# A recommender tower on one core: tile 1's shifted copies of x made on chip like tile 0's, and a new order of the first tiles' loads, turns and lookups

## What is computed

```python
e = stack([tbl_f[ids[:, f]] for f in range(32)], axis=1)       # 1024 x 32 x 16
x0 = h = e
for i in range(3):                                             # W0 128x1024, W1 and W2 128x2048
    z = (x0[:, :, None, :] * h[:, None, :, :]).reshape(B, F * G, E)
    y = relu(einsum('oc,bce->boe', W[i], z) + b[i][None, :, None])
    if i != 2: keep, h = y[:, :64], y[:, 64:]
    else:      keep = y
    xs.append(keep)
z = sum(concatenate(xs, axis=1), axis=2)                       # 1024 x 256
h = concatenate([z, dense_ctx], axis=1)
h = maximum(h @ W_top1 + b_top1, 0); h = maximum(h @ W_top2 + b_top2, 0)
y = h @ W_top3                                                 # 1024 x 1
```

## Time and profile before

| | us |
|---|---|
| median of 3 timed runs | 1061.19 |
| lowest, highest | 1061.14, 1063.73 |
| the profiled execution | 1066.62 |
| its span | 1064.8 |
| TensorE busy in it | 995.8 |
| VectorE busy | 821.8 |
| GpSimd busy | 816.3 |
| ScalarE busy | 474.4 |

### The profile page before, as it was taken

How to read it: one execution, slowest core, us unless ns; L and a number is a source line. 1 busy time by engine, 2 the same in 40 slices (tenths; PEclk the granted TensorE clock), 3 DMA queues, 4 the chain that set the end, 5 groups by cost and what they waited for, 6 DMA issues and landing times.

```text
span 1064.8 us, 11324 instructions
## 1 busy us (share of the span) xinstructions
PE 995.8 (94%) x3089; PEld 572.8 (54%) x3089; DVE 821.8 (77%) x750; ACT 474.4 (45%) x595; POOL 816.3 (77%) x524
## 2 busy tenths in 40 slices
PE   3178899999999999999999999999899999999988
PEld 2133455555555555555555555555455555555565
DVE  6234877798778977899778977898778977788882
ACT  2222544444544454454444454444444454543443
POOL 7655779887998879887998789886998766566540
PEclk9579999999999999999999999999999999999989
DMA  8089999989888888899888888888888888889000
GB/s 158 10 189 198 205 199 190 210 191 197 191 194 191 191 192 185 192 198 208 191 194 186 194 188 190 187 192 191 195 187 188 192 186 192 190 186 219 30 1 0
DMA packets 49012, 185.45 MB, mean 174 GB/s; under 512 B 17570, under 2 KB 22178, under 8 KB 28388
## 3 DMA queue, kind: packets, MB, share of 16 engines
q1 hardware_dynamic: 40804, 183.15, 78.2%
q0 software_dynamic: 8192, 2.11, 2.0%
HBM read 182.06 MB, written 3.15 MB: 174 GB/s over the span
## 4 chain that ended last, share of the span: by engine, by line
POOL 42%; PE 26%; issue 18%; DMA 7%; DVE 4%; ACT 2%; SPq 0%; POOLq 0%; ACTq 0%; DVEq 0%
POOL low L500 24%; POOL looked_up L490 16%; PE y L617 15%; PE y L625 6%; DMA looked_up<-in_tbl,ids_now 4%; PE y L640 3%; POOL tail_parts L508 2%; DMA spread<-xcols 2%; DVE unsplit L1070 1%; DVE prod L1070 1%; DMA xcols<-xrows 0%; ACT emb L793 0%; ACT tail_high L853 0%; PE y L721 0%; DVE acc_kept L1101 0%
## 5 line engine op out<-in xcount | busy, mean ns | idle before, releaser
L500 POOL TENSOR_TENSOR low<-unsplit,high 128x1024 fp32r<-128x1024 f32 x221 | 525.1, 2388 | 113.3 <-ACT high L829 111.5
L617 PE MATMUL y<-prod,w1T 128*128 128x512 f32 x1024 | 480.3, 597 | 5.4 <-ACT kept L821 2.7
L1070 DVE TENSOR_TENSOR prod<-spread,h 128x1024 f32<-128x1024 f32 x288 | 349.1, 1216 | 118.3 <-PE y L617 102.6
L829 ACT CAST high<-unsplit 128x1024 fp32r<-128x1024 f32 x224 | 234.0, 1045 | 243.6 <-DVE unsplit L1070 243.2
L1070 DVE TENSOR_TENSOR unsplit<-spread,h 128x1024 f32<-128x1024 f32 x224 | 272.1, 1215 | 48.8 <-ACT h L815 48.6
L490 POOL DMA_INDIRECT looked_up<-in_tbl,ids_now x256 | 248.7, 971 | 69.1 <-issue 59.4
L617 PEld LDWEIGHTS y<-prod,w1T 128*128 128x128 f32 x1024 | 193.5, 192 | 166.8 <-issue 144.1
L625 PE MATMUL y<-high,w2T_high 128*128 128x512 f32 x448 | 226.7, 506 | 4.4 <-ACT high L829 4.4
L640 PE MATMUL y<-low,w2T_high 128*128 128x512 f32 x448 | 202.7, 533 | 6.3 <-POOL low L500 6.3
L625 PE MATMUL y<-high,w2T_low 128*128 128x512 f32 x448 | 177.9, 397 | 0.0
L815 ACT ACTIVATE h<-y,bias 64x512 f32<-64x512 f32 x128 | 83.3, 651 | 209.2 <-PE y L617 208.3
(11 more groups left out here) (115 smaller groups left out, 441.3 us busy)
## 6 DMA issues: line engine op xcount, KB each, us to landing
spread<-xcols SPq DMA_DIRECT2D x128, 1024.0 KB, 9.0
shifted<-xcols SPq DMA_DIRECT2D x124, 256.0 KB
shifted_tail<-xcols SPq DMA_DIRECT2D x124, 64.0 KB
looked_up<-in_tbl,ids_now POOLq DMA_INDIRECT x256
xcols<-xrows SPq DMA_DIRECT2D x32, 96.0 KB, 2.0
spread<-in_L_rec_W SPq DMA_DIRECT2D x3, 512.0 KB, 7.0
spread<-in_L_rec_W SPq DMA_DIRECT2D x1, 1024.0 KB, 11.6
wt<-in_W_top SPq DMA_DIRECT2D x2, 512.0 KB, 8.7
```

Of the source, the lines that this page charges most:

```text
L500: pool.tensor_tensor(low[kind][r][:, :, :], unsplit[kind][r][:, :, :], high[kind][r][:, :, :].bitcast(F32), ALU.subtract).then_inc(s_low[k ...
L617: last = pe.matmul(y[:, :], w, z[:, c, :], start=(n == 0 and c == 0), stop=(item in (LAST0, LAST1) and c == ITEM - 1))
L829: act.copy(high[kind][r][:, :, :], unsplit[kind][r][:, :, :]).then_inc(s_high[kind], 1)
L1070: dve.tensor_tensor(z, x[:, ITEM * n:ITEM * (n + 1), :], b[:, :].unsqueeze(1).to_broadcast([P, ITEM, COLS]), ALU.mult).then_inc(s_made[kin ...
```

## The change

- Tile 1's `shifted` and `shifted_tail` are made like tile 0's: VectorE rotates, TensorE turns, ScalarE copies, between slots -1 and 0. Tile 2 is the first whose shifted copies come back from DRAM.
- SyncE stores x of tile 1 ahead of tile 0's last spread group, and x of tile 2 between tile 1's first two groups.
- In slot 0 the items (0, 0), TAIL and (0, 1) come earlier, and x of tile 2 is turned after (1, 4) instead of after the last item.
- GpSimd's first tail part comes after four of the eight lookups instead of after all; the second slot's tail part keeps eight ahead of it in all, and the 16 that follow stand in one piece.
- In every fourth slot one lookup moves from before the low part of (2, 5) to after it.
- TensorE turns the identity 8 times ahead of each group of w2, and in a loop 16 times 8 times after the weights are stored. The dense features are turned and stored ahead of w2's groups instead of behind them.

```diff
+IDLE_TURNS, IDLE_LOOPS = 8, 16
...
 EARLY = {-1: [TAIL, (0, 0), (0, 1)],
-         0: [(1, 0), (1, 1), (1, 2), (1, 3), (1, 4), (0, 0), TAIL, (1, 5), (0, 1), (1, 6), (1, 7)]}
+         0: [(1, 0), (1, 1), (0, 0), (1, 2), TAIL, (1, 3), (0, 1), (1, 4), (1, 5), (1, 6), (1, 7)]}
+TURN_AFTER = {-1: (0, 1), 0: (1, 4)}
...
-LOOKUPS_AFTER = ((0, 0, 2, 0, 1, 2, 3), (0, 0, 1, 1, 1, 2, 2))
+LOOKUPS_AFTER = ((0, 0, 2, 0, 0, 3, 3), (0, 0, 1, 1, 1, 2, 2))
 LOOKUPS_FIRST = (0, 1)
+LOOKUPS_BEFORE_TAIL = 4
...
-        unwrapped = flat(spread[1][:, 3:4, :])[:, 0:QUAD * XROWS]
-        rotated = [spread[1][:, 4 + c, :] for c in range(GROUP + 1)]
-        first_shifted = [y1, y2[0], y2[1], h1, h0[1]]
+        FIRST_AT = (3, 9)
+        unwrapped = [flat(spread[1][:, n:n + 1, :])[:, 0:QUAD * XROWS] for n in FIRST_AT]
+        rotated = [[spread[1][:, n + 1 + c, :] for c in range(GROUP + 1)] for n in FIRST_AT]
+
+        first_shifted = [[y1, y2[0], y2[1], h1, h0[1]], [y2[1], h1, h0[1], y2[0], y2[0]]]
         FIRST_ORDER = [GROUP, 0, 1, 2, 3]
...
-            def load_shifted(t):
-
-
+            def store_x(t):
                 sp.wait_ge(s_xrows, number(t) + 1)
                 sp.dma_start(xcols[number(t)], xrows[:, :]).then_inc(s_xcols, 16)
...
             def load_factors(t):
+                store_x(t)
                 load_shifted(t)
-
-                if not isinstance(t[0], int) or number(t) >= 1:
-                    load_spread(after(t, -1), GROUPS - 1)
+                load_spread(after(t, -1), GROUPS - 1)
...
             sp.wait_ge(s_stored, PREP_GROUPS)
-            load_factors((0, 0))
+            store_x((0, 0))
+            sp.wait_ge(s_xcols, 16)
+            for g in range(GROUPS - 1):
+                load_spread((0, 0), g)
+            store_x((0, 1))
+            load_spread((0, 0), GROUPS - 1)
 
             sp.wait_ge(s_dense_parts, 1)
 
-            sp.wait_ge(s_first, len(FIRST_ORDER))
-            load_factors((0, 1))
-            load_factors((0, 2))
+            sp.wait_ge(s_first, 2 * len(FIRST_ORDER))
+            sp.wait_ge(s_xcols, 16 * 2)
+            load_spread((0, 1), 0)
+            store_x((0, 2))
+            load_spread((0, 1), 1)
+            load_shifted((0, 2))
+            for g in range(2, GROUPS):
+                load_spread((0, 1), g)
+            for g in range(GROUPS - 1):
+                load_spread((0, 2), g)
...
             begin(1)
-            for f in range(FIELDS // TILES_PER_BLOCK):
+            for f in range(LOOKUPS_BEFORE_TAIL):
                 look_up(f)
-            for k in range(-1, START):
+            split_tail((0, -1))
+            for f in range(LOOKUPS_BEFORE_TAIL, FIELDS // TILES_PER_BLOCK):
+                look_up(f)
+            split_tail((0, 0))
+            for f in range(FIELDS // TILES_PER_BLOCK, 3 * FIELDS // TILES_PER_BLOCK):
+                look_up(f)
+            for k in range(1, START):
                 slot((0, k))
...
+            def turn_dense():
+                pe.wait_ge(s_dense, 16 * 2 * P // COPY)
+                for b in range(BLOCKS):
+                    last = pe.transpose((y0, y1)[b // GROUP][:, P * (b % GROUP):P * (b % GROUP + 1)], dense_wide[:, b, :],
+                                        ident[:, :])
+                last.then_inc(s_denseT, 1)
+
...
             for g in range(2 * GROUPS):
+                if g == GROUPS:
+                    turn_dense()
                 pe.wait_ge(s_ordered, g // 2 + 1)
+                if g >= GROUPS:
+                    for _ in range(IDLE_TURNS):
+                        pe.transpose(xT[:, 0:P], ident[:, :], ident[:, :])
...
+            with pe.Fori(0, IDLE_LOOPS):
+                for _ in range(IDLE_TURNS):
+                    pe.transpose(xT[:, 0:P], ident[:, :], ident[:, :])
...
-                turn_after = (2, 4) if (2, 4) in items else items[-1]
+                turn_after = (2, 4) if (2, 4) in items else TURN_AFTER.get(number(s))
...
+            def turn_rotated(t, n, c):
+
+                pe.wait_ge(s_rotated, len(FIRST_ORDER) * t + n + 1)
+                for e in range(QUAD):
+                    last = pe.transpose(first_shifted[t][c][:, P * e:P * (e + 1)], rotated[t][c][:, P * e:P * (e + 1)],
+                                        ident[:, :])
+                last.then_inc(s_first, 1)
+
             for n, c in enumerate(FIRST_ORDER):
-                pe.wait_ge(s_rotated, n + 1)
-                for e in range(QUAD):
-                    last = pe.transpose(first_shifted[c][:, P * e:P * (e + 1)], rotated[c][:, P * e:P * (e + 1)], ident[:, :])
-                last.then_inc(s_first, 1)
-            for k in range(-1, START):
+                turn_rotated(0, n, c)
+            slot((0, -1))
+            for n, c in enumerate(FIRST_ORDER):
+                pe.wait_ge(s_first_rows, len(FIRST_ORDER) + (1 if c == 3 else 0))
+                turn_rotated(1, n, c)
+            for k in range(START):
                 slot((0, k))
...
+            def take_first(t):
+                for n, c in enumerate(FIRST_ORDER):
+                    act.wait_ge(s_first, len(FIRST_ORDER) * t + n + 1)
+                    act.copy(shifted_tail[:, :] if c == GROUP else shifted[:, c, :], first_shifted[t][c][:, :]).then_inc(
+                        s_first_rows, 1)
+
+            take_first(0)
+            slot((0, -1))
+
+            act.wait_ge(s_tail, 1)
+            act.wait_ge(s_made[WHOLE], GROUP // ITEM)
+            take_first(1)
+            for k in range(START):
                 slot((0, k))
...
+            def dense_low():
+                dve.wait_ge(s_dense_high, 1)
...
             for n, home in enumerate(homes):
+                if n == 2 + GROUPS:
+                    dense_low()
                 dve.wait_ge(s_turned, n + 1)
...
+            def rotate(t):
+                unwrapped_rows = unwrapped[t].rearrange("p (e w) -> p e w", w=XROWS)
+                for to, fields in ((slice(0, FIELDS), FIELDS), (slice(FIELDS, XROWS), XROWS - FIELDS)):
+                    dve.tensor_copy(unwrapped_rows[:, :, to], emb[:, 0:fields, QUAD * t:QUAD * (t + 1)].rearrange(
+                        "p f e -> p e f")).then_inc(s_unwrapped, 1)
+
+                dve.wait_ge(s_unwrapped, 2 * (t + 1))
+                for c in FIRST_ORDER:
+                    dve.tensor_copy(rotated[t][c].rearrange("p (e a f) -> p e a f", a=GROUP, f=FIELDS),
...
-                if isinstance(s[0], int) and number(s) == -1:
-
-                    dve.wait_ge(s_first_rows, {TAIL: 1, (0, 0): 3, (0, 1): 5}[item])
+                if isinstance(s[0], int) and number(s) < 1 and layer == 0:
+
+                    dve.wait_ge(s_first_rows, len(FIRST_ORDER) * number(t) + {TAIL: 1, (0, 0): 3, (0, 1): 5}[item])
...
-            for k in range(-1, START):
+            dve.wait_ge(s_emb, 1)
+            rotate(0)
+            slot((0, -1))
+            rotate(1)
+            for k in range(START):
                 slot((0, k))
```

More of the change, by code:

```diff
@@ L523, in look_up_some @@
                             look_up(FIELDS // TILES_PER_BLOCK * quarter + left.pop(0))
-                if TAIL in items and not mine:
-                    split_tail(s)
-                if mine:
-                    look_up_some(LOOKUPS_FIRST[quarter > 0])
+                look_up_some(LOOKUPS_FIRST[quarter > 0])
                 for n, item in enumerate(mine):
@@ L568, in _ @@
             for g in range(2 * GROUPS):
+                if g == GROUPS:
+                    turn_dense()
                 pe.wait_ge(s_ordered, g // 2 + 1)
+                if g >= GROUPS:
+                    for _ in range(IDLE_TURNS):
+                        pe.transpose(xT[:, 0:P], ident[:, :], ident[:, :])
                 turn(2 + g, GROUP, P, lambda c: w_turned[g // 2][:, P * (GROUP * (g % 2) + c):P * (GROUP * (g % 2) + c + 1)])
             pe.wait_ge(s_stored, PREP_GROUPS)
-            pe.wait_ge(s_dense, 16 * 2 * P // COPY)
-            for b in range(BLOCKS):
-                last = pe.transpose((y0, y1)[b // GROUP][:, P * (b % GROUP):P * (b % GROUP + 1)], dense_wide[:, b, :],
-                                    ident[:, :])
-            last.then_inc(s_denseT, 1)
+            with pe.Fori(0, IDLE_LOOPS):
+                for _ in range(IDLE_TURNS):
+                    pe.transpose(xT[:, 0:P], ident[:, :], ident[:, :])
             def turn_x(t):
@@ L981, in _ @@
             lows = {2 + GROUPS + g: w2T_low[:, GROUP * g:GROUP * (g + 1), :] for g in range(GROUPS)}
+            def dense_low():
+                dve.wait_ge(s_dense_high, 1)
+                for lanes in (slice(COPY, 2 * COPY), slice(3 * COPY, P)):
+                    for n, bank in enumerate((y0, y1)):
+                        rows = slice(TOP1 * n, TOP1 * (n + 1))
+                        dve.tensor_tensor(dense_parts[lanes, rows], bank[lanes, :], dense_parts[lanes, rows].bitcast(F32),
+                                          ALU.subtract)
```

(8 more changed lines are left out.)

33 lines of the change are left out of this document (6 added, 27 removed).

## The result

| | before | changed |
|---|---|---|
| median of the timed runs, us | 1062.46 (4 runs) | 1050.30 (4 runs) |
| lowest, highest | 1061.14, 1065.91 | 1050.07, 1051.86 |
| the profiled execution, its span | 1066.62, 1064.8 | 1050.27, 1048.4 |
| granted clock of TensorE, mean | 0.976 | 0.993 |

The ratio is 0.9884, with a 95% interval of 0.9869 to 0.9900: 12.2 us faster (1062.46 - 1050.30). The time lies 0.3 us from the 1050.6 predicted, and inside the range. That it is so close is in part luck: 10.6 us had been taken from a median of 1061.19 us, of three runs. A fourth run put that median 1.3 us higher, and the saving was 1.6 us larger.

A forecast was written before the change was run, and what follows sets the result against it. The beginning was taken to hang on transfers and GpSimd's instruction order; slot 1 ending at 119.8 instead of 130.37 us saves 10.6 us, taken from the 1061.19 us median: 1050.6 us, range 1046.5 to 1057.

The forecast's parts named there:

- First tail: GpSimd's first tail low part, after four lookups, starts at 55.6 instead of 59.03 us; TensorE's following product ends 5.5 us earlier.
- Tile 1 on chip: Tile 1 turned on chip frees SyncE's queue: later spread groups and tile 2's `shifted` land 9 to 16 us earlier.
- No VectorE wait on `shifted`: Sign of being right: VectorE's two long waits on `shifted`, 6.53 and 8.13 us in the kernel before, both go.
- The block of 17 lookups: GpSimd between slot 0's tail and slot 1's first low part: lookups end at 91.9 us, TensorE waits some 6 us.
- The low clock: After TensorE's wait in slot 1 the clock falls: 2.3 us lost, bounds 0 and 6; slot 1 ends at 119.8 us.
- Profiled execution against median: Saving from the profiled 1066.62 us carried unchanged to the timed median of 1061.19 us, giving 1050.6 us.
- this lookup: Lookup moved behind (2, 5) every fourth slot: priced at 0, as the rows show no TensorE wait there.
- The turns of the identity: TensorE's 32 turns and loop of 128, under the first lookups: end at 47 to 53 us, no shift taken.
- third rival: Turns never raise the clock, so the loop ends 12 to 17 us after 49.3 us; 1062 to 1067 us, chance 0.05.
- second rival: Loop of turns overruns, from low clock or dear loop turning, ending at 53 to 58 us; 1054.5 to 1059.5, chance 0.18.

The follow-up runs named there:

- second set: Kernel before (1067.27 us) beside two parts of the change alone and two edits of the changed kernel, on another chip; these four took 1069.05 to 1093.49 us.
- third set: Changed kernel again, then without identity turns, also dense stage back, also six lookups more ahead: 1050.77, 1049.86, 1049.99, 1051.03 us; kernel before 1062.91.
- the identity turns alone: Kernel before with only the change's identity turns and early dense stage: 1093.49 us, ratio 1.0237 to the kernel before.
- GpSimd's order alone: Kernel before with only GpSimd's new order: tail behind four lookups, next tail behind eight, then 17 in one piece; 1069.05 us, ratio 1.0018.
- the old order of slot 0: Changed kernel with (0, 0), TAIL and (0, 1) behind (1, 4) again and x of tile 2 turned after (1, 7): 1085.22 us, ratio 1.0161.
- 24 passes: Changed kernel with 24 instead of 16 passes of the loop of identity turns: 1083.51 us, ratio 1.0146 to the kernel before.
- first and third sets: First: changed kernel without identity turns 1050.13 us, first tail after eight lookups 1054.46, four fewer lookups before second tail 1054.55, six more 1049.52; kernel before 1062.98.

## Why the prediction was right, and where it wasn't

*First tail.* Predicted start 55.6 us, measured 54.49, since the turns ahead of it ran at the full clock (55.86 us without the identity turns); the product behind it ended at 58.05 instead of 59.1. Putting the eight lookups back took 4.2 us away.

*Tile 1 on chip and the order of slot 0.* Both long waits on `shifted` went, as said; tile 2's `shifted` was predicted at about 91 us, and VectorE's product with it started at 90.65. "No VectorE wait on `shifted`" did not hold: 1.48 and 2.80 us were left, with no gap of TensorE at either. The order of the items is worth 6 us by the second set's traces. Tile 1's rotated copies were not undone alone, so how these 6 us divide between the order and the copies that allow it was not tried.

*The block of 17 lookups.* Predicted end of the second tail 70.6 us, measured 69.73; end of the wait 94.3, measured 93.27. Both are 0.9 to 1.0 us early because the group landed at 65.3 and not 66.15 us. The wait itself was mis-sized: 2.83 us and not 6. TensorE had been taken as ready at 88.2 us, and came at 90.44: it lost 2.11 us to ScalarE's kept part at 82.39 us, and 1.7 us more to the low clock behind it (eight products in 5.40 us, 3.70 at the full clock). Without these two it would have come at 86.6 us, within the 86 to 88 predicted. The wait on ScalarE is what had been left out, though the kernel before has one of 2.71 us at the same place (93.79 us). This did not change the end, because GpSimd's line set it, as the third set's trace shows.

*The low clock.* One stretch of 2.3 us loss was taken. There were two of 3.4 us, each a loss of 1.7 us: 83.51 to 86.92 us, before the wait and so without effect, and 93.75 to 97.16 us, the only one that counted. Windows of the changed kernel (columns as in rows 1):

```profile
82.00:84.00 2.00, 1.61 (x3) 0.68 (x4) 2.00 (x2) 0.34 (x1) 1.39 (x3) 0.88 1.14 214
84.00:86.00 2.00, 2.00 (x4) 0.93 (x3) 0.31 (x1) 1.04 (x1) 1.54 (x2) 0.50 0.96 187
...
94.00:96.00 2.00, 2.00 (x6) 1.58 (x5) 0.00 (x0) 1.99 (x4) 2.00 (x2) 0.50 1.07 217
```

From 93.27 us the 23.2 us of work left and 1.7 us of lost clock give 118.2 us, and slot 1 ended at 118.40. Predicted were 119.8. The difference of 1.4 us is 1.0 from the landing and 0.6 from the clock, to 0.2 us, so 12.0 us instead of 10.6.

*Profiled execution against median.* The two profiled executions differ by 16.35 us, of which slot 1's end explains 12.0. The other 4.4 lie after it, and 2.6 of them in one late slot, the first of the steady loop's last pass: from one turn of x to the next are 33.26 us in the kernel before (740.71 to 773.97) and 30.68 in the changed one (727.75 to 758.43). These are GpSimd (first row) and TensorE of the kernel before:

```profile
744.01 0.96 POOL L490 DMA_INDIRECT looked_up<-in_tbl,ids_now  x1 [3.80 <-issue]
...
747.39 0.73 PE L640 MATMUL y<-low,w2T_high 128*128 128x512 f32 x2 [1.24 <-POOL low L500]
...
752.18 0.73 PE L640 MATMUL y<-low,w2T_high 128*128 128x512 f32 x2 [1.41 <-POOL low L500]
```

The lookup that starts late is the one that stood ahead of the low part of (2, 5), the one that the change moves behind it; the waits are at (2, 5) and (2, 7). With the next one, of 0.46 us, they come to 3.11 us. The three traces with the old `LOOKUPS_AFTER` (the kernel before, the identity turns alone, GpSimd's order alone) have 3.11, 2.46 and 3.14 us of such waits there, the eleven with the new one 0 to 1.03. The prediction put this lookup at 0, because it saw no wait of TensorE at (2, 5): that was a misreading, and by these rows my estimate of the term is some 2 us. The old list was not put back alone, so this is not shown. It is also open how much of it the timed runs of the kernel before had, of which the profiled one lay 5.4 us above its median. Carrying the saving over to the median unchanged came out well, but the 12.2 us are traced to slot 1's end only as far as one pair of traces goes.

*The turns of the identity.* They cost nothing where the weights are stored in time, and bought nothing, as said. The eight turns behind the dense stage took 1.91 us, the later ones 1.04 to 1.15, and the loop 0.11 us a turn throughout: turns raise the clock and hold it, and turning the loop adds nothing that can be seen. The third rival (turns never raise the clock) is out. The Trainium skill (TensorE: Matmul & The Clock Gate, Part 4) says that the full clock does not engage for transpose-mode work; the trace does not agree for these fp32 turns of the identity, though its rows do not say in which mode they run.

*What was not foreseen.* The second rival, a loop that overruns its cover, had been given a cause inside TensorE. The second set shows it with another one: the cover holds only if VectorE's part of the weights is in time. The changed kernel did not run in that set. An estimate from its rows: with x turned at 77.5 us, as in the kernel with the old order of slot 0, it would be 28 us later than in its own trace, so about 1078 us, against 1067.3 for the kernel before; without the loop 14 to 16 us of that go. That wasn't tried, since the standstill did not return in the third set; so the gain is shown only for runs in which nothing stood still. The cause of the standstill stays open. What the rows say is that it is tied to no place in GpSimd's lookups (with 24 passes the last of the first block starts at 45.02 us and the last of the next four at 53.01, and VectorE went on at 51.60 and 56.62 us; in the kernel with the turns alone it once went on at 45.49), that it is not VectorE's alone (with GpSimd's order alone TensorE had turned the dense features by 43.7 us, and ScalarE cast them only at 50.57), and that no transfer of instructions shows in the trace before 66 us with 24 passes.

## What to carry to other kernels

Where two engines wait for the same beginning by two lines, here transfers and GpSimd's instruction order, move both: GpSimd's order alone gave nothing (1.0018), and with the loads it was part of 1.2%. Price the line that becomes the next one first (here 17 lookups at 1.25 us behind a tail); the size of a wait on it can be wrong by half without moving the end. Filler work that is "hidden" stands in series behind whatever it follows in its engine's order: the 14 us of turns were free and worth nothing in the first and third sets, and 64 more of them cost 7 us where the weights came late. And look for a wait at every place from which work is moved, late slots too: the lookup priced at 0 had one.

## What the runs showed of the hardware

- VectorE stood still for up to 22.4 us at a time in the first 62 us with no event of the program to end it, in all four profiled kernels of the second set and in none of the ten other traces, where the weights were stored by 34 us. ScalarE did so too, for 7.8 us ahead of its dense casts with 24 passes. The same kernel before took 1067.3 us there and 1062.9 to 1063.0 in the other two sets.
- A turn (128x128, fp32) took 0.11 us at the full clock in a loop of eight per pass, with no gap between passes; 128 of them took 14.16 us.
- The clock fell after waits of 2.11 and 2.83 us of TensorE in the changed kernel, each time for 3.4 us; the one of 3.05 us in the earlier trace rows had not brought it down. In the same kernel's trace of the third set the 2.11 us wait did not either, and the one of 3.80 us brought it down, again for 3.4 us (94.9 to 98.3).
- GpSimd idled 3.80 us ahead of one lookup at 744.01 us in the kernel before, with no event of the program to end it (3.03 and 3.77 us at the same place with the identity turns alone and with GpSimd's order alone; in the eleven traces of the new list, where the lookup stands one low part later, at most 1.42).
